# Moving one broadcast DMA from SyncE's queue to ScalarE's, with a reordered SyncE queue and a reordered tail

## The reference

```python
B, N, D = hidden.shape                      # 16, 256, 256
h = _sln(hidden, w, ...)                    # LayerNorm, times gamma(w), plus beta(w)
qkv = (h @ Wqkv.T + bqkv).reshape(B, N, num_heads, hd, 3)
energy = jnp.einsum('bhqd,bhkd->bhqk', q, k)
att = jax.nn.softmax(energy, axis=-1) / D ** 0.5
out = jnp.einsum('bhqk,bhkd->bhqd', att, v)
out = out @ Wp.T + bp
h1 = out + hidden
h2 = _sln(h1, w, ...)                       # the same LayerNorm again
return h2 + h1
```

## Time and profile before

| | |
|---|---|
| median of 3 runs | 350.29 us (349.77 to 354.19) |
| the profiled execution, its own time | 350.8 us |
| its span in the trace | 348.9 us |
| PE busy | 322.5 us (92%) |
| DVE busy | 297.8 us (85%) |
| ACT busy | 239.5 us (69%) |
| POOL busy | 198.5 us (57%) |
| mean granted TensorE clock | 0.98 |
| DMA | 56.90 MB, mean 163 GB/s |

### The profile page before, as it was taken

One profiled execution on the slowest core, in us unless ns is written; L12 is line 12 of the kernel. 1 busy time (PEld: TensorE's weight loads), 2 busy tenths in 40 slices (PEclk: granted clock), 3 DMA queues, 4 the chain that ended last, 5 costly groups with the idle time before them and its releaser, 6 DMA issues.

```text
span 348.9 us, 8808 instructions
## 1 busy us (share of the span) xinstructions
PE 322.5 (92%) x3005; PEld 272.5 (78%) x3005; DVE 297.8 (85%) x689; ACT 239.5 (69%) x476; POOL 198.5 (57%) x243
## 2 busy tenths in 40 slices
PE   7988999997999999999899999999979997997963
PEld 4776879796888888888887887888869896585742
DVE  4888977785999989999899999999969897888881
ACT  7664877776687868686787777787858875556510
POOL 5767271737548474839476583848474543356450
PEclk9899999999999999999999999999999999899996
DMA  8497346676658685977868696967585686524221
GB/s 236 133 210 195 105 124 170 138 199 159 185 141 204 163 221 151 206 190 184 203 141 223 142 225 165 207 161 215 159 214 151 144 209 181 157 29 101 62 60 60
DMA packets 57481, 56.90 MB, mean 163 GB/s; under 512 B 12671, under 2 KB 51342, under 8 KB 57438
## 3 DMA queue, kind: packets, MB, share of 16 engines
q1 hardware_dynamic: 51790, 46.64, 54.8%
q0 software_dynamic: 4464, 8.64, 8.2%
q10 hardware_dynamic: 1184, 1.07, 1.1%
HBM read 9.99 MB, written 4.23 MB: 41 GB/s over the span
## 4 chain that ended last, share of the span: by engine, by line
PE 65%; DMA 15%; DVE 6%; SPq 5%; issue 4%; ACT 1%; POOL 1%; ACTq 1%; DVEq 0%; POOLq 0%
PE m L1074 18%; PE sa L1074 15%; PE st L1074 15%; PE pv L1074 14%; DMA kst<-qk_l 10%; SPq L312 4%; DMA wg<-wb 2%; DVE mx L762 2%; PE m L1206 2%; DMA qst<-m_l 1%; DVE y L897 1%; DMA vrows<-vectors_dram 1%; SPq L325 1%; DVE vare L892 1%; PE pv L1180 1%
## 5 line engine op out<-in xcount | busy, mean ns | idle before, releaser
L762 DVE TENSOR_REDUCE mx<-sa 128x2 f32<-128x512 f32 x256 | 170.7, 680 | 32.8 <-PE sa L1074 27.5
L670 ACT ACTIVATE p<-st 128x512 f32<-128x512 f32 x240 | 140.5, 595 | 41.3 <-PE st L1074 39.2
L1074 PE MATMUL sa<-kst,qst 126*128 126x256 f32 x512 | 106.7, 290 | 11.8 <-DMA kst<-qk_l 9.8
L1074 PE MATMUL st<-qst,kst 128*128 128x256 f32 x496 | 103.8, 292 | 1.4 <-DMA qst<-m_l 0.7
L1074 PEld LDWEIGHTS sa<-kst,qst 126*128 126x128 f32 x512 | 78.8, 190 | 16.6 <-DMA kst<-qk_l 11.9
L1074 PEld LDWEIGHTS st<-qst,kst 128*128 128x128 f32 x496 | 75.3, 188 | 15.7 <-issue 12.9
L406 POOL DMA_DIRECT2D qst<-m_h x31 | 17.6, 569 | 96.9 <-DVE m_l L771 96.7
L1074 PE MATMUL pv<-p,v_st 128*32 128x256 f32 x1008 | 62.3, 388 | 0.0
L1074 PEld LDWEIGHTS pv<-p,v_st 128*32 128x32 f32 x1008 | 29.9, 111 | 21.8 <-issue 3.7
L1074 PE MATMUL m<-hT_h,wqkv_h 128*128 128x256 f32 x128 | 36.1, 295 | 0.7 <-ACT hT_h L684 0.7
L1074 PE MATMUL m<-hT_h,wqkv_l 128*128 128x256 f32 x128 | 34.5, 281 | 0.0
(11 more groups left out here) (153 smaller groups left out, 539.2 us busy)
## 6 DMA issues: line engine op xcount, KB each, us to landing
qst<-qk_h SPq DMA_DIRECT2D x64, 128.0 KB, 3.0
qst<-qk_l SPq DMA_DIRECT2D x64, 128.0 KB, 3.0
kst<-qk_h SPq DMA_DIRECT2D x62, 128.0 KB, 2.8
kst<-qk_l SPq DMA_DIRECT2D x62, 128.0 KB, 2.7
xa<-x_dram SPq DMA_DIRECT2D x16, 256.0 KB, 3.2
gb<-gb_rows POOLq DMA_DIRECT2D x16, 256.0 KB, 5.4
out_dram<-y POOLq DMA_DIRECT2D x15, 256.0 KB, 3.7
wqkv<-oT SPq DMA_DIRECT2D x28, 128.0 KB, 3.7
```

What stands on the lines that cost most here:

```text
L670: nc.scalar.activation(p32[:, h, :], st_ps[h % 2][:], ACT.Exp).then_inc(exp_done, 1)
L762: dve.tensor_reduce(mx[:, par(a), h // HH, (h % HH) * TT:(h % HH + 1) * TT], sa_ps[h % 2][:].rearrange("p (t n) -> p t n", t=TT), AX.X, AL ...
L1074: return nc.tensor.matmul(o, l, r, start=start, stop=stop)
```

## The change

Four things are edited. `spread_rec` is issued by ACT, in slot 14 of step b, after `evict_out(b, 0)` and ahead of that slot's exponential. On SP, `send_out(b, 0)` is no longer the last thing of step b: it comes in step b+1 behind `stack(b + 2, 1)`, just ahead of half 1 of the same batch. On POOL, `low_att` comes after `rstd_out` in slot 5 instead of in slot 4, and after the loop two `send_gb` come ahead of the `send_y` beside them. On DVE, after the loop, `last_out(B - 2, 1)` and `normalise_tokens(B - 2, 1)` come earlier between the stages of `residual(B - 4)`, and `low_att_half(1)` comes ahead of `residual(B - 2, 4)`.

```diff
 # SP
-            def spread_rec(a):
-                ...
-                sp.wait_ge(recs_in, 32 * (a + 1))
-                wait(sp, rows_ready, a)
-                sp.dma_start(o_rec[:], recs...broadcast_to([2 * HH, HD // 2, 2 * N])).then_inc(rec_in, 16)
             def step(b):
                 if has(b - 1) or has(b) and not first(b):
                     stack(b + 1, 1)
-                send_out(b - 1, 1)
+                for g in range(2):
+                    send_out(b - 1, g)
                 ...
-                spread_rec(b - 1)
                 ...
-                send_out(b, 0)
 # POOL, step
-                    if h == 4 and by_transfer(b - 2):
-                        low_att(b - 2)
                     if h == 5 and has(b - 3):
                         rstd_out(b - 3)
+                    if h == 5 and by_transfer(b - 2):
+                        low_att(b - 2)
 # POOL, tail
+            send_gb(B - 2)
             send_y(B - 4)
-            send_gb(B - 2)
             rstd_out(B - 3)
             add_beta(B - 3)
+            send_gb(B - 1)
             send_y(B - 3)
-            send_gb(B - 1)
 # ACT
+            def spread_rec(a):
+                if not by_transfer(a):
+                    return
+                act.wait_ge(recs_in, 32 * (a + 1))
+                wait(act, rows_ready, a)
+                act.dma_start(o_rec[:], recs.rearrange("r (d n) -> r d n", d=1)
+                             .broadcast_to([2 * HH, HD // 2, 2 * N])).then_inc(rec_in, 16)
 # ACT, step, behind evict_out(b, 0) and ahead of the exponential
+                    if h == 14:
+                        spread_rec(b - 1)
 # DVE, tail
             normalise(B - 3)
-            for stage in (1, 2, 3):
+            residual(B - 4, 1)
+            last_out(B - 2, 1)
+            residual(B - 4, 2)
+            normalise_tokens(B - 2, 1)
+            for stage in (3, 4, 5):
                 residual(B - 4, stage)
-            last_out(B - 2, 1)
-            residual(B - 4, 4)
-            normalise_tokens(B - 2, 1)
-            residual(B - 4, 5)
 ...
             low_att_half(0)
+            low_att_half(1)
             residual(B - 2, 4)
-            low_att_half(1)
             residual(B - 2, 5)
```

More of the change, by code:

```diff
@@ L333, in gather_rec @@
                     sp.dma_start(recs[n:2 * HH:2, :], sums[:]).then_inc(recs_in, 16)
-            def spread_rec(a):
-                if not by_transfer(a):
-                    return
-                sp.wait_ge(recs_in, 32 * (a + 1))
-                wait(sp, rows_ready, a)
-                sp.dma_start(o_rec[:], recs.rearrange("r (d n) -> r d n", d=1)
-                             .broadcast_to([2 * HH, HD // 2, 2 * N])).then_inc(rec_in, 16)
             def stack(a, g):
```

## The result

The changed kernel takes 376.18 us (median of 4, 369.02 to 381.56) where the kernel before took 350.98 beside it (median of 4): a ratio of 1.0549, 95% interval 1.0399 to 1.07. By the ratio that is slower by some 19 us, where 346.0 was predicted with 353.0 as the upper end. The ratios here leave disturbed executions out, while the medians count all, so the two differ.

A forecast was written before the change was run, and what follows sets the result against it. PE's 18.2 to 18.3 us per step bounds it, plus waits for a stack's last k part. Slot 8 -3.3, slot 0 -3.3, ACT +2.6, late spread +0.9, tail -1.2 make -4.3 us: 346.0 us, range 340.5 to 353.

The forecast's parts named there:

- PE's floor of 18.2 to 18.3 us: Loop step without a wait for data: PE is busy throughout, so no step can be shorter than 18.2 to 18.3 us.
- The tail: After the loop: PE's 1.21 us wait at the last projection goes, gain 1.2 us, ends 0.8 and 2.
- Slot 0, -3.3 us: Half 0's stack: spread off SP puts its last k part ahead of POOL's y store; half of 6.6 us gained.
- three large cases: Slot 0's PE waits of 2.01, 2.40 and 2.15 us; 6.6 us gained if the order flips in all.
- Half 0's rows: Sums of half 0 leave some 7 us later, but the reciprocals also need half 1's: no cost.
- Slot 8, -3.3 us: Half 1's stack: neither spread nor half 0's rows stand ahead on SP; 3.3 us gained, ends 2.7 and 4.1.
- The gain that I had from the transfers alone (2.7 us): Slot 8's low end: if DMA engines are the limit, only 136 KB of rows leave the stretch, 0.6 us earlier.
- the rival "nothing moves": Loop landings stay since the spread shares engines with the stack; ACT costs 1.5, tail gives 1.2: some 351 us, chance 0.14.
- ACT, +2.6 us: Slot 14: the spread's issue delays exponential 14, costing PE 0.2 us x 13 = 2.6 us, ends 0 and 4.6.
- The slower one, at 355: Rival: competing with eight stack DMAs, the spread lands after 7 us, delaying DVE's normalisation and PE; 355 us, chance 0.16.

The follow-up runs named there:

- the two guarded kernels: Changed kernel, and kernel before with only the spread on ACT, each with ACT waiting for half 0's stack to land before the spread: 376.72 and 368.19 us.
- the 1053 us execution: One of four executions of the kernel before with new tail, reciprocals on every 7th partition and POOL's stores moved to slot 15: 1053.07 us, median 351.73.

## Why the prediction was wrong

**Right.** PE's floor of 18.2 to 18.3 us, and that the waits for the last k part are what moves. The first stack DMA of half 1 does leave 0.03 us behind score 15, in all steps but one. L892 (now L893) takes 0.16 us in the loop. The tail gave 0.9 to 1.1 us of 1.2, although PE's wait at the last projection is 0.49 us and not gone.

**Slot 0, -3.3 us: the step that failed.** I wrote that taking the spread off SP "puts the k part ahead of the store", and looked only at how early the k part leaves. It leaves 0.1 us earlier at the median, not 0.65. This is counted from the start of score 10, in steps 3 to 12: the part leaves after 3.3 to 5.3 us before (median 4.4), after 3.3 to 7.1 in the changed kernel (4.3), and after 3.7 to 5.9 with the spread alone on ACT (4.4). POOL's store goes out after 5.0 us in all three. Score 10 in the timeline of PE, in step 11 of the kernel before (part at 253.94, store at 253.67) and in step 8 of the changed one (part at 205.88, store at 203.83):

```profile
248.65 0.48 PE L1074 MATMUL st<-qst,kst 128*128 128x256 f32 x2
...
198.81 0.48 PE L1075 MATMUL st<-qst,kst 128*128 128x256 f32 x2
```

The spread stood behind the last k part, not ahead of it, so taking it away freed nothing for that part. The store is now ahead of the part in steps 8, 10 and 12, where it was in 11 and 13. And the spread left the one queue in which it had to stay behind: it now leaves from 0.65 us ahead of the part to 1.7 behind. The slot-0 waits went from 6.8 to 17.4 us (3.09, 5.03, 4.47, 3.86, 0.96), +10.6 where -3.3 stood. One of my three large cases was misread as well: in the step of the wait of 2.01 us no store goes out, and what leaves ahead of the k part (at 82.50) is POOL's load of gamma and beta, at 81.99.

**Half 0's rows: "Free".** I followed the data (who needs the sums) and not the queue. The rows now stand on SP ahead of the x load and of all of `stack(b + 2, 0)`, while POOL's store follows its own time; more k parts come at or behind it. Alone this costs some 9 us (1.0253, 1.0016 to 1.049).

**Slot 8, -3.3 us.** The waits there went from 4.06 to 5.04 us (0.90, 1.87, 0.88, 0.73 and 0.66, at 120 to 243 us). The stack of half 1 starts earlier, but now its own issues are stretched, here the first two:

```profile
187.21 2.54 SPq L312 DMA_DIRECT2D qst<-qk_h  x2
```

Two issues take 1.2 us where nothing holds them. The spread still runs at that time (185.70 to 191.43), and so does POOL's store (to 190.19), so a stack issue on SP is stretched although ACT issued the spread. The gain that I had from the transfers alone (2.7 us) and the rival "nothing moves" were nearer, but the waits grew by 1.0 us, which neither had.

**ACT, +2.6 us: it is about nothing.** The issue runs beside an operation that ACT has begun:

```profile
185.53 0.60 ACT L671 ACTIVATE p<-st 128x512 f32<-128x512 f32 x1 [0.23 <-PE st L1075]
185.70 0.55 ACTq L613 DMA_DIRECT2D wg<-wb  x1
186.03 0.59 ACT L605 ACTIVATE oT<-pv 128x512 f32<-128x512 f32 x1
186.50 1.31 ACT L671 ACTIVATE p<-st 128x512 f32<-128x512 f32 x2
```

In 12 of the 14 steps the exponential starts before `evict_out` has ended. In two it starts 0.34 and 1.13 us behind it; at the second, at 205.23, the gather is probably the cause, since SP issued its second part only at 203.24. The weight loads of the scores wait 1.3 us for exponentials in all, 1.5 before.

**The rivals.** The slower one, at 355, named the wrong victim: the spread itself. It lands after 4.7/5.8/6.3 us (shortest, median, longest), and DVE waits for it 0.6 us in all. The victim is the transfer that competes with it, which I had measured at 4.2 us and never asked what more load would do to. None of my cases had the clock either: a wait of 2.40 us left it at 1.00, and I took a wait's price to be its length. The same trace had the other case, behind the wait of 2.15 us that ends at 296.37 (columns as in the earlier trace rows):

```profile
297.70:301.10 3.40, 3.40 (x30) 1.80 (x34) 3.07 (x7) 0.66 (x3) 0.99 (x2) 0.50 0.75 194
```

**Still open.** Why three landings in the two guarded kernels took over 5 us with the spread held back, what the order costs once the spread is fast, and the 1053 us execution. Why long and quiet steps alternate is only argued: a long step gives the queued transfers time to drain (DMA share 0.49 to 0.54 in the quiet ones behind a long one), so the next k part lands at once.

## What to carry to other kernels

Before a DMA is moved to another engine's queue, list what stands directly ahead of it in the old one: here one queue kept a big slow transfer behind a small urgent one, and a second queue did not. Price a landing under the new neighbours, not by its median. And when a transfer is slow for its bytes, mend its rate before its place: spacing 16 source rows gave 2.5% (3.2% with a step of 7 and the new tail), and every order tried without it gave nothing or a loss.

## What the runs showed of the hardware

- A broadcast of 256 KB from 16 neighbouring partitions took seven bins of 0.35 us at 94 to 127 GB/s with the DMA engines busy; from every 8th partition four bins at 166 to 211, from every 7th three at 225, 328 and 173.
- Behind waits of 3.09, 5.03 and 3.86 us PE ran at a granted 0.50 for 5.8, 6.1 and 5.9 us, behind one of 4.47 us for 2.9. Behind waits of 2.15 and 2.36 us the clock fell to 0.50 1.3 and 0.9 us after PE had resumed, for 3.4 us; behind one of 2.40 us it stayed at 1.00. With half of the time at 0.50 counted as lost, the wait of 5.03 us cost 1.6 times its length and that of 3.09 us 1.9 times.
- Two issues of stack DMAs on SP, 1.2 us where nothing holds them, took 2.54 us at 187.21 and 3.24 us at 207.45 in the changed kernel, while the spread that ACT had issued and POOL's DMAs were in flight.
- A DMA issue on ACT cost its arithmetic nothing where an operation was already running: the issue of 0.55 us at 185.70 overlaps two operations that follow each other without a gap.
